# A two-layer network and a wide sigmoid head on one core: another order of the start, of the loop's small steps, and of the gathers

## The chip, the core and the metric

The kernel runs on one core of a Trainium2 chip. A core has TensorE (PE, matrix products), VectorE (DVE), ScalarE (ACT), GpSimd (POOL) and SyncE (SP), each with its own in-order program, and 16 DMA engines that they share. Engines wait for each other by semaphores. The metric is device time in microseconds (us) of one execution; less is better.

## The reference

For each of 2048 pairs (user, item) the kernel gathers two embeddings of 32 numbers, runs two layers of 128 with a relu, and makes 1250 logits. The one-hot part of the head is a lookup of a row of the head's matrix by item.

```
all_embed = jnp.concatenate([users_emb_w[users], items_emb_w[items]], axis=1)
h = jax.nn.relu(all_embed @ w1.T + b1)
h = jax.nn.relu(h @ w2.T + b2)
cross = jax.nn.one_hot(items, NUM_ITEMS, dtype=h.dtype)
head_in = jnp.concatenate([cross, h], axis=1)
return jax.nn.sigmoid(head_in @ w_head.T + b_head)
```

## The kernel before, in words

The 2048 pairs are 16 tiles of 128 (`TILES`, `LAST` = 15). The host lays an item's embedding and its row of the head side by side, so that one gathered item row has 1282 numbers.

**POOL** makes the identity `ident` and then issues for each tile two indirect DMAs: the item rows (L181, 128 x 1282 numbers) and the user rows (L185, 128 x 32). Both raise the tile's own semaphore `s_rows[t]`; a tile's embedding is complete when both have landed. From tile 4 on POOL waits for tile t-4 to have landed.

**The steps of a tile t.** Products run in fp32r, a format of reduced precision, so operands are split into a high and a low part.
- DVE `split_emb(t)` (cast L221, subtract L223) makes `emb`, high and low side by side; it waits for `s_rows[t]`.
- PE `transpose(t)` (L340) writes `ps_x`; DVE `copy_embT(t)` (L227) copies it to `embT`.
- PE `layer_1(t)` (L345, L346); ACT `relu_1(t)` (L296) makes `h1T`; PE `layer_2(t)` (L355); ACT `relu_2(t)` makes `h2T_hi` (L300) and `h2T_f` (L305); DVE `split_h2(t)` (L231) makes `h2T_lo`.
- PE's head in four passes over 1250 columns (512, 512, 226) into `acc[t % 2]` in PSUM: bias (`bias_sel` x `bias_parts`), high (`h2T_hi` x `w_hid_hi`), high-low (`h2T_hi` x `w_hid_lo`), low (`h2T_lo` x `w_hid_hi`). All are L359. The end of the low pass raises `s_acc`. Tiles 0, 14 and 15 go bank by bank instead (`bank_head`, L385 to L390), with `s_bank_acc` after each bank.
- DVE `add_part(t, i)` (L244) adds `acc` to the gathered head row, in two halves of 625 for tiles 1 to 13 (`HALVED`), in three banks otherwise. ACT `sigmoid(t, i)` (L310) follows in place, and SP stores the part (L166).

**The order** of each engine's program is written out by hand. PE has a loop over tiles 2 to 13 (`Fori`, two tiles a turn): bias pass of t, layer 1 of t+1, high pass and high-low pass of t, layer 2 of t+1, transpose of t+2, low pass of t. The programs of DVE and ACT are unrolled Python loops whose order fits this.

**The start.** PE multiplies zeros (`WARM` = 6 products of 512 columns, L395). SP loads `idx`, the head's bias, `w1T` twice and `w2T`; ACT loads b1, b2 as columns of one number per partition, and `w_hid_f` (625 KB), which ACT copies and DVE splits into `w_hid_hi` and `w_hid_lo` (`split_hidden(i)`, L213).

Of the kernel before, what the change touches and what calls it, by code (L numbers as in the profile page):

```python
# [8 lines left out]
IN_FLIGHT = 4  # L9
WARM = 6  # L10
HALVED = tuple(range(1, 14))
STORED_WHOLE = (9, 10, 11)

ALU = mybir.AluOpType
# [6 lines left out]
def rec_head_kernel(nc, pairs, user_rows, item_rows, w1T, b1, w2T, b2, w_hiddenT, b_head, out):  # L21
# [15 lines left out]
    BANKS = len(chunks)  # L37
    SPARE = BANKS * BANK - P

# [13 lines left out]
    assert B % P == 0 and H1 == P and H2 == P and 2 * K1 == P and item_rows.shape[1] == ITEM_ROW  # L53
    assert BP * BC == N and TILES > IN_FLIGHT and SPARE >= N and LAST % 2 == 1

# [6 lines left out]
    with ExitStack() as ctx:  # L62
# [6 lines left out]
        def sem(name):  # L69
            return ctx.enter_context(nc.semaphore(name))  # L70
# [7 lines left out]
        w2T_sb = sb("w2T_sb", [H1, H2], F32)  # L78
        b1_sb = sb("b1_sb", [H1, 1], F32)
        b2_sb = sb("b2_sb", [H2, 1], F32)  # L80
        w_hid_f = sb("w_hid_f", [H2, N], F32)
# [55 lines left out]
        def second_layer(t):  # L137


            return acc[1][:, SPARE:SPARE + P] if t == 0 else ps_h[:, P:2 * P]  # L140

# [8 lines left out]
        @block.sync  # L150
        def _(sp):
            sp.dma_start(idx[:], pairs_v).then_inc(s_idx, 16)
            sp.dma_start(bias_f[:], bias_v).then_inc(s_bhead, 16)
            for half in range(2):
                sp.dma_start(w1T_f[half * K1:(half + 1) * K1, :], w1T).then_inc(s_w1, 16)
            sp.dma_start(w2T_sb[:], w2T).then_inc(s_w2, 16)
            sp.wait_ge(s_const, 3)
            sp.wait_ge(s_bias_split, 2)
            for r, part in enumerate((bias_hi, bias_lo)):
                sp.dma_start(bias_parts[r:r + 1, :].bitcast(F32).rearrange("a (p c) -> a p c", p=BP),  # L160
                             part[:].bitcast(F32)).then_inc(s_bias_row, 16)

            for t in range(TILES):
                for i, (c, n) in enumerate(stores[t][:-1] if t == LAST else stores[t]):
                    sp.wait_ge(s_prob, parts_until(t) if t in STORED_WHOLE else parts_until(t - 1) + i + 1)
                    sp.dma_start(out_v[:, t * N + c:t * N + c + n], logits(t, c, n)).then_inc(s_out, 16)  # L166
            sp.wait_ge(s_out, 16 * sum(len(s) for s in stores))

        @block.gpsimd
        def _(pool):  # L170
            nc.gpsimd.memset(ident[:], 0.0).then_inc(s_zero, 1)
            pool.wait_ge(s_zero, 1)
            nc.gpsimd.affine_select(out=ident[:], in_=ident[:], compare_op=ALU.not_equal, fill=1.0, base=0,
                                    pattern=[[-1, P]], channel_multiplier=1).then_inc(s_ident, 1)
            pool.wait_ge(s_idx, 16)
            for t in range(TILES):

                if t >= IN_FLIGHT:
# [4 lines left out]
                    in_offset=bass.IndirectOffsetOnAxis(ap=idx[:, 2 * t + 1:2 * t + 2], axis=0),  # L183
                ).then_inc(s_rows[t], 16)
                nc.gpsimd.indirect_dma_start(  # L185
                    out=rows[:, at:at + UD], out_offset=None, in_=user_rows,
                    in_offset=bass.IndirectOffsetOnAxis(ap=idx[:, 2 * t:2 * t + 1], axis=0),
                ).then_inc(s_rows[t], 16)

        @block.vector  # L190
        def _(dve):
            nc.vector.memset(warm_pe[:], 0.0).then_inc(s_warm_pe, 1)  # L192
            nc.vector.memset(warm[:], 0.0).then_inc(s_const, 1)
# [64 lines left out]
            split_h2(1)
            add_part(0, 1)
            add_part(0, 2)  # L260
            split_emb(3)
            copy_embT(3)
# [18 lines left out]
        def _(act):  # L281


            act.dma_start(b1_sb[:], b1.rearrange("(p a) -> p a", a=1)).then_inc(s_b12, 16)
            act.dma_start(b2_sb[:], b2.rearrange("(p a) -> p a", a=1)).then_inc(s_b12, 16)
            act.dma_start(w_hid_f[:], w_hiddenT).then_inc(s_hidden, 16)
            act.wait_ge(s_const, 1)
# [6 lines left out]
            def relu_1(t):  # L294
                act.wait_ge(s_l1, t + 1)
                nc.scalar.activation(h1T[:], ps_h[:, 0:P], ACT.Relu, bias=b1_sb[:]).then_inc(s_h1, 1)  # L296

            def relu_2(t):
                act.wait_ge(s_l2, t + 1)
                nc.scalar.activation(h2T_hi[t % SLOTS][:], second_layer(t), ACT.Relu,  # L300
                                     bias=b2_sb[:]).then_inc(s_h2_hi, 1)
                if t >= 1:

                    act.wait_ge(s_h2_lo, t)
                nc.scalar.activation(h2T_f[:], second_layer(t), ACT.Relu, bias=b2_sb[:]).then_inc(s_h2, 1)  # L305

# [4 lines left out]

            act.wait_ge(s_b12, 32)
            relu_1(0)
            relu_2(0)
            relu_1(1)
            relu_2(1)
            sigmoid(0, 0)
            relu_1(2)
            sigmoid(0, 1)
            relu_2(2)  # L320
            sigmoid(0, 2)
# [15 lines left out]
        def _(pe):  # L337
# [40 lines left out]

            def bank_head(t, i):

                s = t % SLOTS
                c, n = chunks[i]
                if t >= SLOTS:
                    pe.wait_ge(s_sum, parts_until(t - SLOTS))
                    nc.tensor.matmul(acc[s][:, c:c + n], bias_sel[:], bias_parts[:, c:c + n], start=True, stop=False)  # L385
                pe.wait_ge(s_h2_hi, t + 1)
                nc.tensor.matmul(acc[s][:, c:c + n], h2T_hi[s][:], w_hid_hi[:, c:c + n], start=False, stop=False)  # L387
                nc.tensor.matmul(acc[s][:, c:c + n], h2T_hi[s][:], w_hid_lo[:, c:c + n], start=False, stop=False)  # L388
                pe.wait_ge(s_h2_lo, t + 1)
                nc.tensor.matmul(acc[s][:, c:c + n], h2T_lo[s][:], w_hid_hi[:, c:c + n],  # L390
                                 start=False, stop=True).then_inc(s_bank_acc, 1)

            pe.wait_ge(s_warm_pe, 1)
# [12 lines left out]
            layer_2(0, second_layer(0))  # L406
            transpose(1)

            pe.wait_ge(s_h1, 1)
            layer_1(1)  # L410
            bank_head(0, 0)
            layer_2(1)
            bank_head(0, 1)
            transpose(2)

            bias_pass(1, chunks[-1:])
            bank_head(0, 2)
            def small_beside_head(t, s):
                next_layer_1(t + 1)
                hi_pass(t, s)  # L420
                hi_lo_pass(s)

                layer_2(t + 1)
                transpose(t + 2)
                lo_pass(t, s)

            small_beside_head(1, 1)

            with pe.Fori(1, LAST // 2) as i:
                for s in range(SLOTS):  # L430
# [3 lines left out]
                    one_pass(s, bias_sel[:], bias_parts, True, False)  # L434
                    small_beside_head(t, s)
# [39 lines left out]
```

## Time and profile before

| what | value |
|---|---|
| median of the runs | 66.62 us (66.48 to 66.84, 3 runs) |
| span of the profiled execution, first to last instruction | 65.9 us |
| PE busy | 56.0 us (85%) |
| DVE busy | 43.0 us (65%) |
| ACT busy | 40.3 us (61%) |
| POOL busy | 31.2 us (47%) |
| moved by DMA | 21.85 MB, mean 332 GB/s |

The span is what the hardware profiler saw on the core. The execution's own time is not given beside it, so the runs' median is set against it: about 0.7 us more. Busy times overlap between engines.

### The profile page before, as it was taken

How to read it: one execution, taken by the hardware profiler on the slowest of the kernel's cores; microseconds unless marked ns; L12 is line 12 of the kernel's file. 1: busy time of each engine (PE TensorE's matmuls, PEld its weight loads, DVE VectorE, ACT ScalarE, POOL GpSimd, SP SyncE). 2: the span in 40 equal slices, each digit the busy share in tenths (PEclk: the TensorE clock that was granted, in tenths of full speed). 3: DMA queues.
4: the chain of work that ended last, by engine and by line, in shares of the span. 5: the costliest groups of instructions: out<-in, count | busy, mean ns of one | idle time of the engine just before them, and what ended most of it. 6: DMA issues, size and time to landing. Idle time of an engine off the chain costs nothing.

```text
span 65.9 us, 958 instructions
## 1 busy us (share of the span) xinstructions
PE 56.0 (85%) x284; PEld 44.9 (68%) x284; DVE 43.0 (65%) x111; ACT 40.3 (61%) x91; POOL 31.2 (47%) x38
## 2 busy tenths in 40 slices
PE   1999909799999999999999999999999999993000
PEld 1344207388888888888888888888888878881000
DVE  3811666134558987978879797887978879966000
ACT  0623931424256787777878768787876878978000
POOL 4287688688688678768768868800000000000000
PEclk9999998555599999999999999999999999999955
DMA  0489998998989899999999999999999999999940
GB/s 0 53 321 291 298 350 257 222 343 259 222 283 303 336 382 401 392 406 409 401 410 414 400 426 411 410 413 415 410 402 395 419 404 401 390 346 346 372 145 9
DMA packets 8367, 21.85 MB, mean 332 GB/s; under 512 B 1580, under 2 KB 2476, under 8 KB 8364
## 3 DMA queue, kind: packets, MB, share of 16 engines
q0 software_dynamic: 2816, 10.77, 46.7%
q1 hardware_dynamic: 4972, 10.29, 41.1%
q10 hardware_dynamic: 576, 0.76, 3.8%
q8 instruction: 1, 0.02, 0.1%
q14 instruction: 2, 0.02, 0.1%
HBM read 11.56 MB, written 10.24 MB: 331 GB/s over the span
## 4 chain that ended last, share of the span: by engine, by line
PE 73%; DMA 11%; ACT 2%; DVE 2%; POOL 2%; issue 2%
PE acc L359 47%; DMA rows<-user_rows,idx 8%; PE ps_h L355 6%; PE acc L387 3%; PE acc L390 3%; PE acc L388 3%; PE ps_x L340 3%; PE ps_h L346 3%; DMA idx<-pairs 3%; PE ps_h L345 3%; PE acc L385 2%; POOL rows L181 2%; ACT rows L310 1%; DVE rows L244 1%; PE acc L355 1%
## 5 line engine op out<-in xcount | busy, mean ns | idle before, releaser
L244 DVE TENSOR_TENSOR rows<-acc,rows 128x625 f32<-128x625 f32 (+2 forms) x35 | 25.8, 749 | 5.3 <-PE acc L359 3.2
L310 ACT ACTIVATE rows<-rows 128x625 f32<-128x625 f32 (+2 forms) x35 | 23.3, 678 | 0.9 <-DVE rows L244 0.9
L181 POOL DMA_INDIRECT rows<-item_rows,idx x16 | 15.3, 954 | 6.0 <-issue 4.6
L185 POOL DMA_INDIRECT rows<-user_rows,idx x16 | 15.3, 955 | 4.9 <-issue 4.9
L359 PE MATMUL acc<-bias_parts,bias_sel 128*128 128x512 f32 (+1 forms) x42 | 11.2, 373 | 0.0
L359 PE MATMUL acc<-w_hid_hi,h2T_lo 128*128 128x512 f32 (+1 forms) x39 | 10.5, 376 | 0.0
L296 ACT ACTIVATE h1T<-ps_h,b_sb 128x128 f32<-128x128 f32 x16 | 5.9, 368 | 7.1 <-PE ps_h L346 6.6
L359 PE MATMUL acc<-w_hid_hi,h2T_hi 128*128 128x512 f32 (+1 forms) x39 | 10.0, 365 | 0.0
L300 ACT ACTIVATE h2T_hi<-ps_h,b_sb 128x128 fp32r<-128x128 f32 x15 | 5.5, 369 | 7.1 <-PE ps_h L355 7.1
L359 PE MATMUL acc<-w_hid_lo,h2T_hi 128*128 128x512 f32 (+1 forms) x39 | 9.6, 354 | 0.0
L227 DVE CAST embT<-ps_x 128x128 fp32r<-128x128 f32 x16 | 4.7, 292 | 5.5 <-PE ps_x L340 5.4
L395 PE MATMUL ps_x<-warm_pe 128*128 128x512 f32 x12 | 6.8, 728 | 1.5 <-DVE warm_pe L192 1.5
L359 PEld LDWEIGHTS acc<-bias_parts,bias_sel 128*128 128x128 f32 x42 | 7.0, 194 | 1.2 <-issue 0.2
L359 PEld LDWEIGHTS acc<-w_hid_lo,h2T_hi 128*128 128x128 f32 x39 | 6.3, 189 | 1.1
L359 PEld LDWEIGHTS acc<-w_hid_hi,h2T_hi 128*128 128x128 f32 x39 | 6.4, 190 | 0.5
L359 PEld LDWEIGHTS acc<-w_hid_hi,h2T_lo 128*128 128x128 f32 x39 | 6.4, 190 | 0.5
L340 PE MATMUL ps_x<-ident,emb 128*128 128x128 f32 x16 | 4.7, 292 | 1.8 <-DVE emb L223 1.8
L355 PE MATMUL ps_h<-h1T,w2T_sb 128*128 128x128 f32 x30 | 6.1, 287 | 0.0
L395 PEld LDWEIGHTS ps_x<-warm_pe 128*128 128x128 f32 x12 | 2.8, 241 | 4.7 <-issue 3.2
L355 PEld LDWEIGHTS ps_h<-h1T,w2T_sb 128*128 128x128 f32 x30 | 4.9, 199 | 0.9
L305 ACT ACTIVATE h2T_f<-ps_h,b_sb 128x128 f32<-128x128 f32 x15 | 5.4, 363 | 0.0
L231 DVE TENSOR_TENSOR h2T_lo<-h2T_f,h2T_hi 128x128 fp32r<-128x128 f32 x16 | 4.6, 290 | 0.5 <-ACT h2T_f L305 0.4
(39 smaller groups left out, 58.1 us busy)
## 6 DMA issues: line engine op xcount, KB each, us to landing
probs<-rows SPq DMA_DIRECT2D x20, 312.5 KB
probs<-rows SPq DMA_DIRECT2D x3, 625.0 KB
probs<-rows SPq DMA_DIRECT2D x6, 256.0 KB
w_hid_f<-w_hiddenT ACTq DMA_DIRECT2D x1, 625.0 KB
rows<-item_rows,idx POOLq DMA_INDIRECT x16, 5.9
rows<-user_rows,idx POOLq DMA_INDIRECT x16, 5.9
probs<-rows SPq DMA_DIRECT2D x2, 113.0 KB
probs<-rows ACTq DMA_DIRECT2D x1, 113.0 KB
```

Of the source, the lines that this page charges most:

```text
L181: nc.gpsimd.indirect_dma_start(out=rows[:, at + UD:at + ROW], out_offset=None, in_=item_rows, in_offset=bass.IndirectOffsetOnAxis(ap=idx[: ...
L185: nc.gpsimd.indirect_dma_start(out=rows[:, at:at + UD], out_offset=None, in_=user_rows, in_offset=bass.IndirectOffsetOnAxis(ap=idx[:, 2 * ...
L227: nc.vector.tensor_copy(embT[:], ps_x[:, 0:P]).then_inc(s_embT, 1)
L244: nc.vector.tensor_tensor(logits(t, c, n), acc[t % SLOTS][:, c:c + n], logits(t, c, n), ALU.add).then_inc(s_sum, 1)
L296: nc.scalar.activation(h1T[:], ps_h[:, 0:P], ACT.Relu, bias=b1_sb[:]).then_inc(s_h1, 1)
L300: nc.scalar.activation(h2T_hi[t % SLOTS][:], second_layer(t), ACT.Relu, bias=b2_sb[:]).then_inc(s_h2_hi, 1)
L305: nc.scalar.activation(h2T_f[:], second_layer(t), ACT.Relu, bias=b2_sb[:]).then_inc(s_h2, 1)
L310: nc.scalar.activation(logits(t, c, n), logits(t, c, n), ACT.Sigmoid).then_inc(s_prob, 1)
L340: nc.tensor.transpose(ps_x[:, 0:P], emb[:], ident[:]).then_inc(s_xT, 1)
L355: nc.tensor.matmul(sums, w2T_sb[:], h1T[:], start=True, stop=True).then_inc(s_l2, 1)
L359: last = nc.tensor.matmul(acc[s][:, c:c + n], h, w[:, c:c + n], start=first, stop=end)
L395: nc.tensor.matmul(ps_x[:], warm_pe[:, 0:P], warm_pe[:], start=True, stop=True)
```

## The change

- **POOL.** The load of `w_hid_f` is issued first, by POOL and not by ACT; the memset of `ident` goes to DVE. From tile 3 on (`ITEM_FIRST`) the item gather of tile t+1 is issued ahead of the user gather of tile t.
- **Loads.** One half of `w1T` and the head's bias go from SP to ACT. b1 and b2 come in as two rows, are transposed by one small product into `ps_h`, and copied by DVE into `b12_sb`.
- **PE's start.** 3 long warm-up products, and 4 and 3 short ones of 128 columns after the first and second part of `w_hid_hi`. Bias products of tile 0 fill the time until `embT`, and its bias pass runs again after layer 1. The second layer of tile 0 goes to `ps_x`. Tile 0's head and the small steps of tile 1 are interleaved anew, with the low product of a bank apart (`bank_lo`).
- **The loop, PE.** Layer 1 of t+1 stands behind the high pass of t.
- **The loop, DVE.** Copy, first add, h2 split, second add, then the embedding split of t+2, which stood between the first add and the h2 split.
- **The loop, ACT.** The first sigmoid stands ahead of relu 1, the second ahead of relu 2, up to tile 12.
- **Before the last tiles.** Bank 0 of tile 14 stands ahead of layer 1 of tile 15, bank 1 ahead of layer 2.

```diff
-WARM = 6
+WARM = 3
+WARM_SHORT = (4, 3)
+ITEM_FIRST = 3
@@ sync
-            sp.dma_start(bias_f[:], bias_v).then_inc(s_bhead, 16)
-            for half in range(2):
-                sp.dma_start(w1T_f[half * K1:(half + 1) * K1, :], w1T).then_inc(s_w1, 16)
+            sp.dma_start(w1T_f[0:K1, :], w1T).then_inc(s_w1, 16)
@@ gpsimd
-            nc.gpsimd.memset(ident[:], 0.0).then_inc(s_zero, 1)
+            pool.dma_start(w_hid_f[:], w_hiddenT).then_inc(s_hidden, 16)
...
+            for t in range(TILES):
+                if t < ITEM_FIRST:
+                    item_gather(t)
+                if t + 1 >= ITEM_FIRST and t < LAST:
+                    item_gather(t + 1)
+                user_gather(t)
@@ vector
+            dve.wait_ge(s_b12_T, 1)
+            nc.vector.tensor_copy(b12_sb[:], ps_h[:, 0:2]).then_inc(s_b12_sb, 1)
...
             for t in range(2, LAST - 1):
-
+                copy_embT(t + 1)
                 add_part(t - 1, 0)
-                if t + 2 < TILES:
-                    split_emb(t + 2)
                 split_h2(t)
                 add_part(t - 1, 1)
-                if t + 2 < TILES:
-                    copy_embT(t + 2)
+                split_emb(t + 2)
+            copy_embT(LAST)
+            add_part(LAST - 2, 0)
             split_h2(LAST - 1)
-            add_rows(LAST - 2)
+            add_part(LAST - 2, 1)
@@ scalar
-            act.dma_start(w_hid_f[:], w_hiddenT).then_inc(s_hidden, 16)
+            act.dma_start(w1T_f[K1:2 * K1, :], w1T).then_inc(s_w1, 16)
+            act.dma_start(bias_f[:], bias_v).then_inc(s_bhead, 16)
+            act.dma_start(b12_rows[0:1, :], b1.rearrange("(a p) -> a p", a=1)).then_inc(s_b12, 16)
+            act.dma_start(b12_rows[1:2, :], b2.rearrange("(a p) -> a p", a=1)).then_inc(s_b12, 16)
...
-            for t in range(2, LAST):
-
+            for t in range(2, LAST - 2):
+                sigmoid(t - 1, 0)
                 relu_1(t + 1)
-
+                sigmoid(t - 1, 1)
+                relu_2(t + 1)
+            for t in (LAST - 2, LAST - 1):
                 sigmoid(t - 1, 0)
+                relu_1(t + 1)
                 relu_2(t + 1)
                 sigmoid(t - 1, 1)
@@ tensor
             pe.wait_ge(s_warm_pe, 1)
-            for _ in range(WARM):
-                nc.tensor.matmul(ps_x[:], warm_pe[:, 0:P], warm_pe[:], start=True, stop=True)
+            warm_up(WARM, BANK)
             pe.wait_ge(s_ident, 1)
+            pe.wait_ge(s_b12, 32)
+            nc.tensor.transpose(ps_h[:, 0:2], b12_rows[:], ident[0:2, 0:2]).then_inc(s_b12_T, 1)
+            for bank, count in enumerate(WARM_SHORT):
+                pe.wait_ge(s_hid_hi, bank + 1)
+                warm_up(count, P)
             transpose(0)
-            pe.wait_ge(s_w1_parts, 2)
-
             pe.wait_ge(s_const, 4)
             pe.wait_ge(s_bias_row, 32)
+            one_pass(0, bias_sel[:], bias_parts, True, True, chunks[:-1])
+            pe.wait_ge(s_w1_parts, 2)
+            layer_1(0)
             bias_pass(0)
-            layer_1(0)
-            bias_pass(1, chunks[:-1])
             pe.wait_ge(s_w2, 16)
             layer_2(0, second_layer(0))
+            bias_pass(1)
+            bank_hi(0, 0)
...
+                    hi_pass(t, s)
+                    next_layer_1(t + 1)
+                    hi_lo_pass(s)
+                    layer_2(t + 1)
+                    transpose(t + 2)
+                    lo_pass(t, s)
+            bank_head(LAST - 1, 0)
             next_layer_1(LAST)
-            bank_head(LAST - 1, 0)
+            bank_head(LAST - 1, 1)
             layer_2(LAST)
-            bank_head(LAST - 1, 1)
```

On DVE in the loop, from one first add to the next, the kernel before has these rows (`rows<-acc,rows` is an add, `emb` the embedding split):

```order
L244 TENSOR_TENSOR rows<-acc,rows 128x625
L221 CAST emb<-rows 128x64
L223 TENSOR_TENSOR emb<-rows,emb 128x64
L231 TENSOR_TENSOR h2T_lo<-h2T_f,h2T_hi 128x128
L244 TENSOR_TENSOR rows<-acc,rows 128x625
L227 CAST embT<-ps_x 128x128
```

The changed kernel has these, at the same place:

```order
L256 TENSOR_TENSOR rows<-acc,rows 128x625
L243 TENSOR_TENSOR h2T_lo<-h2T_f,h2T_hi 128x128
L256 TENSOR_TENSOR rows<-acc,rows 128x625
L233 CAST emb<-rows 128x64
L235 TENSOR_TENSOR emb<-rows,emb 128x64
L239 CAST embT<-ps_x 128x128
```

The two instructions of the embedding split have moved behind both adds.

On ACT in the loop, from one `h1T` (relu 1) on, before:

```order
L296 ACTIVATE h1T<-ps_h,b_sb 128x128
L310 ACTIVATE rows<-rows 128x625
L300 ACTIVATE h2T_hi<-ps_h,b_sb 128x128
L305 ACTIVATE h2T_f<-ps_h,b_sb 128x128
L310 ACTIVATE rows<-rows 128x625
```

and in the changed kernel, from one first sigmoid (`rows<-rows`) on:

```order
L321 ACTIVATE rows<-rows 128x625
L307 ACTIVATE h1T<-ps_h,b_sb 128x128
L321 ACTIVATE rows<-rows 128x625
L311 ACTIVATE h2T_hi<-ps_h,b_sb 128x128
L316 ACTIVATE h2T_f<-ps_h,b_sb 128x128
```

Each relu now has a sigmoid of the tile before ahead of it.

## Rows read from the trace of the kernel before

**Rows 1.** The page: the span, then PE's granted clock and DMA in 40 slices.

```profile
span 65.9 us, 958 instructions
...
PEclk9999998555599999999999999999999999999955
DMA  0489998998989899999999999999999999999940
```

**Rows 2.** Two stretches: length, busy time by engine, granted clock, DMA share, GB/s.

```profile
20.00:48.00 28.00, 28.00 (x171) 24.66 (x169) 23.52 (x60) 21.67 (x50) 17.41 (x19) 1.00 1.03 397
48.00:60.00 12.00, 11.74 (x67) 9.82 (x65) 9.91 (x23) 9.85 (x22) 0.00 (x0) 1.00 1.01 388
```

**Rows 3.** Timeline of one period in the loop: start, length, engine, instruction.

```profile
26.06 0.81 DVE L244 TENSOR_TENSOR rows<-acc,rows 128x625 f32<-128x625 f32 x1 [0.27 <-PE acc L359]
...
26.79 0.18 DVE L221 CAST emb<-rows 128x64 fp32r<-128x64 f32 x1
26.82 0.37 ACT L296 ACTIVATE h1T<-ps_h,b_sb 128x128 f32<-128x128 f32 x1 [0.18 <-PE ps_h L346]
...
27.00 0.23 DVE L223 TENSOR_TENSOR emb<-rows,emb 128x64 f32<-128x64 f32 x1
27.08 0.72 ACT L310 ACTIVATE rows<-rows 128x625 f32<-128x625 f32 x1
27.15 0.29 DVE L231 TENSOR_TENSOR h2T_lo<-h2T_f,h2T_hi 128x128 fp32r<-128x128 f32 x1
...
27.35 0.81 DVE L244 TENSOR_TENSOR rows<-acc,rows 128x625 f32<-128x625 f32 x1
...
28.03 0.27 PE L340 MATMUL ps_x<-ident,emb 128*128 128x128 f32 x1
...
28.34 0.29 DVE L227 CAST embT<-ps_x 128x128 fp32r<-128x128 f32 x1 [0.19 <-PE ps_x L340]
...
28.90 0.81 DVE L244 TENSOR_TENSOR rows<-acc,rows 128x625 f32<-128x625 f32 x1 [0.27 <-PE acc L359]
```

**Rows 4.** Timeline: warm-up, the transposes of tiles 0 and 3.

```profile
1.46 6.82 PE L395 MATMUL ps_x<-warm_pe 128*128 128x512 f32 x12 [1.46 <-DVE warm_pe L192]
...
9.67 0.22 DVE L223 TENSOR_TENSOR emb<-rows,emb 128x64 f32<-128x64 f32 x1
...
10.04 0.30 PE L340 MATMUL ps_x<-ident,emb 128*128 128x128 f32 x1 [1.77 <-DVE emb L223]
...
19.51 0.27 PE L340 MATMUL ps_x<-ident,emb 128*128 128x128 f32 x1
```

**Rows 5.** The chain that ended last: users of tile 0, two products of 512 columns.

```profile
4.31 5.11 DMA rows<-user_rows,idx
...
14.43 0.43 PE acc L388
...
55.44 0.23 PE acc L388
```

**Rows 6.** DMA issues from 11.8 to 11.9 us: the last number is us to landing.

```profile
rows<-user_rows,idx POOLq DMA_INDIRECT x1, 3.5
```

**Rows 7.** Timeline: the transpose of tile 15 and the end.

```profile
53.59 0.27 PE L340 MATMUL ps_x<-ident,emb 128*128 128x128 f32 x1
...
60.12 0.91 ACT L310 ACTIVATE rows<-rows 128x512 f32<-128x512 f32 x2 [0.29 <-DVE rows L244]
61.06 0.35 ACTq L334 DMA_DIRECT2D probs<-rows  x1
```

**Rows 8.** Waits of SP's queue: total, times, longest.

```profile
SPq L62 <- DMA probs<-rows: 4.4, 1, 4.4
```

**Rows 9.** DMA issues from 0.7 to 0.8 us.

```profile
idx<-pairs SPq DMA_DIRECT2D x1, 16.0 KB, 1.9
```

**Rows 10.** Waits from 54 to 66 us.

```profile
PEld ps_h L345 <- ACT h2T_f L305: 0.3, 1, 0.3
```

**Rows 11.** DMA issues from 19.2 to 19.5 us (users of tile 6).

```profile
rows<-user_rows,idx POOLq DMA_INDIRECT x1, 5.9
```

**Rows 12.** DMA issues from 40.6 to 40.8 us (items of tile 15).

```profile
rows<-item_rows,idx POOLq DMA_INDIRECT x1, 7.8
```

More of the change, by code:

```diff
@@ L53, in rec_head_kernel @@
     assert B % P == 0 and H1 == P and H2 == P and 2 * K1 == P and item_rows.shape[1] == ITEM_ROW
-    assert BP * BC == N and TILES > IN_FLIGHT and SPARE >= N and LAST % 2 == 1
+    assert BP * BC == N and TILES > IN_FLIGHT and LAST % 2 == 1
     assert all(parts_until(t) == 2 * t + 3 for t in range(LAST - 1))
@@ L107, in rec_head_kernel @@
         s_b12 = sem("s_b12")
+        s_b12_T = sem("s_b12_T")
+        s_b12_sb = sem("s_b12_sb")
         s_hidden = sem("s_hidden")
@@ L175, in _, with item_gather @@
             pool.wait_ge(s_idx, 16)
-            for t in range(TILES):
+            def item_gather(t):
                 if t >= IN_FLIGHT:
@@ L184, in _, with user_gather @@
                 ).then_inc(s_rows[t], 16)
+            def user_gather(t):
+                at = t * ROW
                 nc.gpsimd.indirect_dma_start(
@@ L188, in _ @@
                 ).then_inc(s_rows[t], 16)
+            for t in range(TILES):
[4 more added lines that the diff above has]
+                user_gather(t)
         @block.vector
         def _(dve):
+            nc.vector.memset(ident[:], 0.0).then_inc(s_zero, 1)
             nc.vector.memset(warm_pe[:], 0.0).then_inc(s_warm_pe, 1)
@@ L295, in relu_1 @@
                 act.wait_ge(s_l1, t + 1)
-                nc.scalar.activation(h1T[:], ps_h[:, 0:P], ACT.Relu, bias=b1_sb[:]).then_inc(s_h1, 1)
+                nc.scalar.activation(h1T[:], ps_h[:, 0:P], ACT.Relu, bias=b12_sb[:, 0:1]).then_inc(s_h1, 1)
             def relu_2(t):
@@ L300, in relu_2 @@
                 nc.scalar.activation(h2T_hi[t % SLOTS][:], second_layer(t), ACT.Relu,
-                                     bias=b2_sb[:]).then_inc(s_h2_hi, 1)
+                                     bias=b12_sb[:, 1:2]).then_inc(s_h2_hi, 1)
                 if t >= 1:
                     act.wait_ge(s_h2_lo, t)
-                nc.scalar.activation(h2T_f[:], second_layer(t), ACT.Relu, bias=b2_sb[:]).then_inc(s_h2, 1)
+                nc.scalar.activation(h2T_f[:], second_layer(t), ACT.Relu, bias=b12_sb[:, 1:2]).then_inc(s_h2, 1)
             def sigmoid(t, i):
@@ L391, in bank_head, with warm_up @@
                                  start=False, stop=True).then_inc(s_bank_acc, 1)
+            def bank_head(t, i):
+                if t >= SLOTS:
+                    bank_bias(t, i)
+                bank_hi(t, i)
+                bank_lo(t, i)
+            def warm_up(count, cols):
+                for _ in range(count):
+                    nc.tensor.matmul(acc[0][:, 0:cols], warm_pe[:, 0:P], warm_pe[:, 0:cols], start=True, stop=True)
             pe.wait_ge(s_warm_pe, 1)
-            for _ in range(WARM):
-                nc.tensor.matmul(ps_x[:], warm_pe[:, 0:P], warm_pe[:], start=True, stop=True)
+            warm_up(WARM, BANK)
             pe.wait_ge(s_ident, 1)
+            pe.wait_ge(s_b12, 32)
[3 more added lines that the diff above has]
+                warm_up(count, P)
             transpose(0)
-            pe.wait_ge(s_w1_parts, 2)
             pe.wait_ge(s_const, 4)
             pe.wait_ge(s_bias_row, 32)
+            one_pass(0, bias_sel[:], bias_parts, True, True, chunks[:-1])
+            pe.wait_ge(s_w1_parts, 2)
+            layer_1(0)
             bias_pass(0)
-            layer_1(0)
-            bias_pass(1, chunks[:-1])
             pe.wait_ge(s_w2, 16)
             layer_2(0, second_layer(0))
+            bias_pass(1)
+            bank_hi(0, 0)
+            pe.wait_ge(s_h2, 1)
             transpose(1)
-            pe.wait_ge(s_h1, 1)
+            bank_lo(0, 0)
+            bank_hi(0, 1)
             layer_1(1)
-            bank_head(0, 0)
+            bank_lo(0, 1)
+            bank_hi(0, 2)
+            bank_lo(0, 2)
             layer_2(1)
-            bank_head(0, 1)
+            hi_pass(1, 1)
             transpose(2)
[L416 to L427, printed above, removed]
+            hi_lo_pass(1)
+            next_layer_1(2)
+            lo_pass(1, 1)
+            layer_2(2)
+            transpose(3)
             with pe.Fori(1, LAST // 2) as i:
```

46 lines of the change are left out of this document (24 added, 22 removed).

## The prediction

> **What bounds the kernel now.** I read the page first. Its span is 65.9 us [rows 1], and the runs have a median of 66.62, so 0.7 us lie around the span; all sums below are made on the span and 0.7 is added at the end. The DMA line stands at 9 from the third slice almost to the end, and the TensorE line is at full clock but for four slices near the start and the last two [rows 1]. The windows then tell the two main stages apart. From 20 to 48 us PE is busy for the whole 28 us, and the DMA engines too (share 1.03, 397 GB/s) [rows 2]. So two things are full at once. PE takes one tile per 2.84 us (two adds of the same half of successive tiles start at 26.06 and 28.90 [rows 3]). A tile moves 128 x 1282 x 4 + 128 x 32 x 4 bytes in and 128 x 1250 x 4 out, 1.31 MB, which is 3.3 us at 397 GB/s. So until the gathers are through, PE makes output faster than it is stored and a backlog of stores grows; after that the stores have the engines alone (48 to 60 us: PE 11.74 of 12, DMA 1.01) [rows 2]. At the end both meet: ACT's last sigmoids end at 61.03 (60.12 + 0.91), its store is issued at 61.06, and SP waits 4.4 us for stores [rows 7, 8]; the span ends at 65.9, 4.87 us after the last sigmoid. That is more than twice the 1.9 us that a small lone transfer takes from issue to landing (idx) [rows 9], so some of it is backlog.
>
> For the timetable I use three marks of PE: the transpose of tile 0 at 10.04, of tile 3 at 19.51 [rows 4], of tile 15 at 53.59 [rows 7]. 19.51 + 12 x 2.84 = 53.59. The last sigmoid comes 7.44 later.
>
> **The change, part by part.** The largest part is the order in the loop, where I find a ring of waits. In the changed loop DVE goes copy, first add, h2 split, second add, embedding split (cast and subtract), and PE puts the transpose of tile t+2, which needs that embedding split, ahead of the low pass of tile t, whose end releases the next first add. All of it is now one after the other. Its length from [rows 3], start to start: first add 0.73 (26.06 to 26.79), h2 split 0.20 (27.15 to 27.35), second add 0.73 (as the first, same shape), cast 0.21 (26.79 to 27.00), subtract 0.23. The release of PE after a subtract took 0.14 to 0.15 (at tile 0: cast and subtract done at 9.89, transpose 10.04 [rows 4]). Together 2.25 from the first add to the transpose. From the transpose to the next first add it is 0.87 (28.03 to 28.90). The ring is 3.12 us. Before, the embedding split stood between the first add and the h2 split and was done by 27.23, 0.8 us before PE wanted it at 28.03; PE's own work, 2.84, was the longer.
>
> A second ring on ACT is nearly as long: the first sigmoid now stands ahead of relu 1. First add 0.81, then 0.03, sigmoid about 0.62 to the next start, relu 1 0.37, 0.05 to 0.13 to PE, layer 2 0.23, and 0.87 back: 2.98 to 3.06. It stays just behind the first. Moving layer 1 behind the high pass costs nothing, since relu 1 waits for the sigmoid anyhow.
>
> The ring acts from tile 4 to tile 15. The first period is shorter, since the low pass of tile 1 still stands ahead of the transpose of tile 3: 2.8. So tile 3 to tile 15 takes 2.8 + 11 x 3.12 = 37.1 against 34.1: **+3.0 us**.
>
> The tail: the low pass of bank 0 of tile 14 now waits for an h2 split that stands behind the add of tile 13. That split ends at 0.87 + 0.73 + 0.29 = 1.89 after the last transpose, PE goes on at 2.02, having arrived at 1.40. The stall of 0.6 replaces one of 0.3 that PE has there now (its weight load's wait for h2T_f) [rows 10]. +0.3, so 7.8 from the last transpose to the last sigmoid.
>
> The start. The new order there reaches the first add earlier by work that PE leaves for later, and what counts for the end is when tile 3 is transposed. PE warms up with 3 long products in place of 6 (now it works without a break from 1.46 to 8.28 [rows 4]) and with 7 short ones. The page shows the granted clock at half from 11.5 to 18 us after PE had stood idle for 1.77 us ahead of tile 0 [rows 1, 4]; a product of 512 columns then takes 0.43, against 0.23 at full clock [rows 5]. With less work ahead of tile 0 than now I expect half clock there too, and take it to last until the transpose of tile 1; that is a choice between full clock throughout (first rival) and half clock until tile 3, which would add 1.5 us. The Trainium skill (TensorE: Matmul & The Clock Gate, Part 1) states that the low clock is the default and activity lifts it; by that rule too fewer warm-up products are a risk, and the page's slices agree. Steps from the transpose of tile 0, at half clock: two bias products 0.86, layer 1 at 0.98 to 1.41, three bias products 1.06, layer 2 0.43, three more 1.06, two of bank 0 0.86: transpose of tile 1 at +4.8. From there at full clock: three bank passes and layer 1 and 2 of tile 1, 1.8; to relu 2 of tile 1 and through it 0.9; high pass 0.58, transpose and high-low pass 0.7, layer 1 0.2, relu 1 0.7, layer 2 0.23: +5.2. So tile 3 comes 10.0 us after tile 0.
>
> When is tile 0 transposed? Its rows landed 5.11 us after the issue of the users at 4.31 [rows 5], where the users of tile 3, asked for at 11.84, took 3.5 [rows 6]; the large load of w_hid shares the engines in between. That load now goes through POOL's queue ahead of the gathers. The bounds are 1.6 us earlier (5.11 less 3.5) and 1.6 later (0.64 MB at 397 GB/s wholly in front). POOL itself waits for idx with time to spare either way. I take 0.3 earlier, near none, since load and gather move the same bytes as before. Tile 0 at 9.7, tile 3 at 19.7 (now 19.51).
>
> The items of tile t+1 ahead of the users of tile t: POOL issues just as many gathers, items are asked for one slot (1.25 us) earlier and users one slot later, from tile 2 on. Users of tile 3: asked at 13.09, 3.5 to land, 16.6; wanted by 19. Users of tile 6, asked at 19.33 now, take 5.9 [rows 11]: now 25.2, then 26.5, wanted at 28.1 (19.7 + 2.8 + 2 x 3.12 less 0.6). 1.6 us of cover, so I cost it at nothing. If the cover is gone, DVE stands at the cast, and the adds behind it stand too. The gain from it, earlier bytes, is in the drain, which is not last here.
>
> b1 and b2 as two rows, a transpose of two columns and a copy: beside the wait for w_hid and the gathers, nothing. The memset of ident moves to DVE, about 0.2 us, ahead of waits that are longer: nothing.
>
> The sum: 19.7 + 37.1 + 7.8 = 64.6 for the last sigmoid (now 61.03). Behind it, between 2.2 (0.3 to issue and the 1.9 of a lone transfer) and today's 4.87 [rows 7, 9]. PE now makes a tile in 3.12 us and the stores alone need 0.64 MB / 388 GB/s = 1.65, so after the gathers the backlog melts: about 5.9 MB are left at 48 us, 15 us of work, done near 63, before the last sigmoid. I take 2.9. Span 67.5, time 68.2. (The Trainium skill, DMA: Bandwidth & Descriptors, "Anatomy of one DMA", gives about 2.0 us fixed and bytes / 436 GB/s. By it the last store of 0.12 MB takes 2.3, with 0.3 ahead 2.6, and the time is 67.9, called an estimate.)
>
> **The rivals.** (1) The clock stays full from the warm-up on. For it: long products at 10.2 us still ran at full clock after a pause of 1.77; against it: the clock fell soon after, and there will be less work in that stretch. Then tile 3 comes 8.4 after tile 0, 18.1, the last sigmoid at 63.0, the drain near 63.3 takes part again: span 66.2, time 66.9. (2) Late users. If gathers fall back by a slot more than I take, as the last item gather does (7.8 us [rows 12], where 5.9 left 1.6 of cover), each tile waits for the next tile's items: +1, 69.2. (3) Faster, the other side: the ring does not bind, because DVE gets through its steps faster when it works them off in this order, and the end stays with the drain. Then the earlier items fill the gaps in the gathers between 10 and 18 us (DMA line at 8 to 9 [rows 1]) and the drain ends 0.6 to 1 us earlier: 65.8. It decides if the ring is shorter than about 2.9 us, for 19.7 + 12 x 2.9 + 7.8 = 62.3 ends no later than the drain lets it. All its pieces are measured, so I give it little.
>
> **How the numbers follow.** The main case 0.46 (68.2, its own range 67.3 to 69.1), full clock 0.24 (66.9, half of it within 0.5%), late users 0.16 (69.2), no ring 0.14 (65.8). 0.5%, 0.33 us, is about what a measurement can tell. Faster: the last case and a little of the second, 0.16. Same: 0.14. Slower: 0.70. The range leaves out the fast case and the far end of late users: 66.3 to 69.4.
>
> **What would show it.** In the loop, first adds 3.1 us apart, PE idle some 0.28 before each transpose with the subtract as releaser, PE busy near 91% there. The transposes of tiles 3 and 15 near 19.7 and 56.8, the last sigmoid near 64.6. PEclk at half around tile 0. DMA below 9 in the last slices. Adds 2.84 apart would refute the ring; casts that wait for user rows would show late users.

## The result, and the profile after

The changed kernel takes **69.51 us** (median of 4 runs, 68.63 to 70.03) against 66.69 in the same job, with a ratio of 1.0377 (95% interval 1.0308 to 1.0446). The ratios, here and below, are those of the fast runs alone, while the medians have the slow runs in them, so differences between kernels are read from the ratios. By the medians the change costs 2.8 us, by the ratio 2.5. The forecast was 68.2 with a range up to 69.4: the sign was right and the size too small. The median lies 0.1 us above the range, the time by the ratio (66.69 x 1.0377 = 69.2) inside it.

The page of the changed kernel, the same lines as [rows 1]:

```profile
span 67.7 us, 982 instructions
...
PEclk9999999999999999999999999999999999999999
DMA  0589999999989999999999999999999775544990
```

This execution took 69.57 us, so 1.87 lie around its span. PE's clock never falls to its half level. The DMA line drops to 7, 5 and 4 before the end, where that of before stood at 9.

The two stretches of [rows 2]:

```profile
20.00:48.00 28.00, 27.88 (x154) 22.40 (x153) 21.39 (x55) 19.72 (x45) 17.09 (x18) 1.00 1.02 398
48.00:60.00 12.00, 11.60 (x66) 9.25 (x64) 8.88 (x22) 7.94 (x18) 0.00 (x0) 1.00 0.80 314
```

From 20 to 48 us the DMA engines are as full as before. PE has 154 instructions recorded there against 171, DVE 55 against 60, and yet PE reads as busy for 27.88 us. Part of the waiting is counted into the products' durations (a product of layer 2 reads as 326 ns on average there, 278 before), so PE's busy share hides the ring; the numbers of instructions show it, and so does the busy time of the weight loads (22.40 against 24.66). From 48 us on the stores no longer fill the DMA engines (0.80 against 1.01): the drain now has slack, and what PE loses is lost at the end too.

One period of the loop, as [rows 3] (timeline):

```profile
25.64 0.81 DVE L256 TENSOR_TENSOR rows<-acc,rows 128x625 f32<-128x625 f32 x1 [0.28 <-PE acc L373]
...
26.48 0.73 ACT L321 ACTIVATE rows<-rows 128x625 f32<-128x625 f32 x1 [0.89 <-DVE rows L256]
26.57 0.80 DVE L256 TENSOR_TENSOR rows<-acc,rows 128x625 f32<-128x625 f32 x1
27.12 0.35 ACT L307 ACTIVATE h1T<-ps_h,b_sb 128x128 f32<-128x128 f32 x1
27.29 0.18 DVE L233 CAST emb<-rows 128x64 fp32r<-128x64 f32 x1
27.50 0.23 DVE L235 TENSOR_TENSOR emb<-rows,emb 128x64 f32<-128x64 f32 x1
27.52 0.49 PE L369 MATMUL ps_h<-h1T,w2T_sb 128*128 128x128 f32 x2
27.84 0.27 PE L354 MATMUL ps_x<-ident,emb 128*128 128x128 f32 x1
28.73 0.81 DVE L256 TENSOR_TENSOR rows<-acc,rows 128x625 f32<-128x625 f32 x1 [0.28 <-PE acc L373]
```

First adds are 3.09 apart (25.64, 28.73), 2.84 before. Both rings can be read off. On DVE: add, add, cast, subtract to 27.73, transpose at 27.84, next add at 28.73. On ACT: add to 26.45, sigmoid at 26.48, relu 1 at 27.12 to 27.47, layer 2 at 27.52. They end within 0.1 us of each other: the transpose follows layer 2 by 0.32, about what it takes where no subtract is late (0.33 in a kernel below, 36.72 to 37.05), and it follows the end of the subtract by 0.11. The waits name the one on ACT (engine, line, what for: total, times, longest):

```profile
ACT rows L321 <- DVE rows L256: 11.0, 13, 1.1
...
POOL rows L180 <- DMA rows<-user_rows,idx: 3.8, 6, 1.1
...
PEld ps_h L369 <- ACT h1T L307: 3.4, 12, 0.4
```

The start (timeline; `bias_parts` holds the head's bias, `bias_f` is its load):

```profile
1.34 0.92 ACTq L295 DMA_DIRECT2D bias_f<-b_head  x1
...
4.45 0.45 DVE L209 CAST bias_hi<-bias_f 10x125 fp32r<-10x125 f32 x1 [1.20 <-DMA bias_f<-b_head]
...
6.23 0.73 SPq L159 DMA_DIRECT2D bias_parts<-bias_lo  x1
...
9.12 0.33 PE L354 MATMUL ps_x<-ident,emb 128*128 128x128 f32 x1 [0.50 <-DVE emb L235]
...
10.78 0.70 PE L373 MATMUL acc<-bias_parts,bias_sel 128*128 128x512 f32 x2 [1.34 <-DMA bias_parts<-bias_lo]
11.33 0.22 PE L359 MATMUL ps_h<-embT,w1T_hi 128*128 128x128 f32 x1
...
13.77 0.27 PE L354 MATMUL ps_x<-ident,emb 128*128 128x128 f32 x1
...
18.92 0.27 PE L354 MATMUL ps_x<-ident,emb 128*128 128x128 f32 x1
```

Here is a wait that I had not looked for. Between the transpose of tile 0 (9.12) and everything else PE stands 1.34 us for `bias_parts`. The chain that ended last goes through it:

```profile
1.34 3.08 DMA bias_f<-b_head
4.45 0.46 DVE bias_hi L209
5.31 0.87 SPq L159
6.23 4.42 DMA bias_parts<-bias_lo
```

The end, as [rows 7], and SP's last wait, as [rows 8]:

```profile
55.90 0.27 PE L354 MATMUL ps_x<-ident,emb 128*128 128x128 f32 x1
...
60.27 3.59 ACT L321 ACTIVATE rows<-rows 128x625 f32<-128x625 f32 x7
63.89 0.38 ACTq L348 DMA_DIRECT2D probs<-rows  x1
```

```profile
SPq L63 <- DMA probs<-rows: 3.3, 1, 3.3
```

Tile 15 is transposed at 55.90, the last sigmoid ends at 63.86, and the span at 67.7, 3.84 later (4.87 before).

### The profile page after: what moved, and what is told of

Its sections match the earlier page's. It is cut to its first block, busy times and chain, and to the rows that moved or that the text cites. A ratio compares the mean times of both kernels' runs of the same rounds, so it can differ in the third digit from the quotient of the medians.

```text
span 67.7 us, 982 instructions
## 1 busy us (share of the span) xinstructions
PE 58.2 (86%) x295; PEld 44.2 (65%) x295; DVE 43.7 (64%) x113; ACT 39.9 (59%) x91; POOL 31.6 (47%) x38
## 4 chain that ended last, share of the span: by engine, by line
PE 67%; DMA 11%; DVE 8%; ACT 4%; SPq 1%; issue 1%; ACTq 1%
PE acc L373 45%; PE ps_h L369 9%; DMA bias_parts<-bias_lo 7%; DVE rows L256 6%; DMA bias_f<-b_head 5%; PE ps_x L354 3%; PE ps_h L360 2%; ACT rows L321 2%; PE acc L413 2%; PE ps_h L359 2%; PE acc L403 1%; SPq L159 1%; PE acc L407 1%; ACT h2T_hi L311 1%; ACTq L294 1%
## 5 line engine op out<-in xcount | busy, mean ns | idle before, releaser
L373 PE MATMUL acc<-w_hid_lo,h2T_hi 128*128 128x512 f32 (+1 forms) x39 | 10.2, 370 | 0.0
L424 PE MATMUL acc<-warm_pe 128*128 128x128 f32 (+1 forms) x20 | 6.9, 505 | 1.6 <-DVE warm_pe L202 1.6
L369 PE MATMUL ps_h<-h1T,w2T_sb 128*128 128x128 f32 x30 | 7.2, 322 | 0.1
L424 PEld LDWEIGHTS acc<-warm_pe 128*128 128x128 f32 x20 | 3.5, 232 | 3.7 <-issue 2.1
```

The lines of the kernel that those rows point to most:

```text
L369: nc.tensor.matmul(sums, w2T_sb[:], h1T[:], start=True, stop=True).then_inc(s_l2, 1)
L373: last = nc.tensor.matmul(acc[s][:, c:c + n], h, w[:, c:c + n], start=first, stop=end)
L424: nc.tensor.matmul(acc[0][:, 0:cols], warm_pe[:, 0:P], warm_pe[:, 0:cols], start=True, stop=True)
```

## The experiments

Twelve runs in three jobs. "T3" and "T15" are the transposes of those tiles in the profiled execution, in us; period is the usual distance of transposes in the middle of the loop. The first row is from the job of the result; in the two other jobs of this table the kernel before had a median of 66.64.

| kernel | median us | ratio to before | T3 | T15 | period |
|---|---|---|---|---|---|
| changed | 69.51 | 1.0377 (1.0308 to 1.0446) | 18.92 | 55.90 | 3.08 |
| changed, old gather order | 68.78 | 1.0368 (1.0308 to 1.0428) | 20.04 | 56.91 | 3.08 |
| changed, old ACT order | 69.21 | 1.0387 (1.0312 to 1.0462) | 18.27 | 55.12 | 3.08 |
| changed, old DVE order | 69.51 | 1.0405 (1.032 to 1.049) | 18.36 | 55.73 | 3.09 |
| changed, old ACT and DVE | 68.30 | 1.028 (1.0214 to 1.0345) | 19.50 | 54.91 | 2.96 |
| changed, old PE, ACT, DVE loops | 67.91 | 1.0186 (1.0125 to 1.0247) | 19.34 | 54.70 | 2.85 |
| before, looked at again | 66.43 (one run) | none | 16.95 | 52.48 | 2.84 |
| before, new PE, ACT, DVE loops | 67.23 | 1.011 (1.0068 to 1.0153) | 16.72 | 54.38 | 3.08 |
| before, items first | 66.39 | 0.9966 (0.9935 to 0.9998) | 19.98 | 54.56 | 2.85 |

**The gather order alone, undone.**

```diff
-ITEM_FIRST = 3
+ITEM_FIRST = 16
```

> The changed kernel with the old order of gathers (items and users of a tile one after the other). Theory (the loop's ring of waits costs, the gathers' order does not): adds of the loop stay 3.09 us apart, tile 15 transposed within 0.5 us of 55.9, time 69.3 to 69.8. Rival (users behind the next items make each tile late): 1 us or more faster, below 68.6.

68.78 against 69.51, below the 69.3 to 69.8 expected, but with ratios whose intervals nearly coincide: no difference can be told. Adds and transposes are as far apart as before the edit. Tiles 3 and 15 are late in the table because the profiled execution (70.54 us) was granted only half clock, 0.50 from 12 to 14 us: tile 1 comes 5.89 us after tile 0 there, against 4.65, and tile 15 36.87 after tile 3, against 36.98. The new waits of POOL's item gathers for rows (3.8 us in the changed kernel, above) are gone here, and nothing came of it: POOL was ahead. No cost and no gain of items-first can be seen in this kernel.

**One ring undone, then the other, then both.**

```diff
 ACT, tiles 2 to 12 (first edit)
-                sigmoid(t - 1, 0)
                 relu_1(t + 1)
-                sigmoid(t - 1, 1)
+                sigmoid(t - 1, 0)
                 relu_2(t + 1)
+                sigmoid(t - 1, 1)
 DVE, tiles 2 to 13 (second edit)
                 add_part(t - 1, 0)
+                split_emb(t + 2)
                 split_h2(t)
                 add_part(t - 1, 1)
-                split_emb(t + 2)
```

> The changed kernel with ACT's old order in the loop (relu 1 ahead of the first sigmoid, relu 2 ahead of the second), DVE as changed. If the ring through DVE is as long as worked out, the period is still 3.05 to 3.12 and the time 69.2 to 69.7. If only the ring through ACT binds, the period falls to 2.85 and the time by 2 us or more.

> The changed kernel with DVE's old place for the embedding split (behind the first add), ACT as changed. If the ring through ACT binds too, the period stays at 3.05 to 3.09 and the time at 69.2 to 69.6. If only the ring through DVE binds, the period falls to 2.85 and the time by 2 us or more.

> The changed kernel with both old orders in the loop, all else as changed. Theory of the rings: period 2.84 to 2.90, tile 15 transposed 2 to 2.8 us earlier than 55.9, and the time falls by 1.5 to 2.8 us to 66.7 to 68; it falls by less than PE wins if stores are last by then. Rival (start, tail or what lies around the span is what costs): within 0.5 us of 69.5.

Either edit alone leaves the period at 3.08 or 3.09 and the time where it was (medians 69.21 and 69.51, ratios 1.0387 and 1.0405 against 1.0377). In the timeline the binding ring changes. With the old ACT order PE has layer 2 done early and the transpose follows the subtract:

```profile
46.76 0.81 DVE L256 TENSOR_TENSOR rows<-acc,rows 128x625 f32<-128x625 f32 x1 [0.28 <-PE acc L373]
...
48.51 0.49 PE L369 MATMUL ps_h<-h1T,w2T_sb 128*128 128x128 f32 x2
48.62 0.23 DVE L235 TENSOR_TENSOR emb<-rows,emb 128x64 f32<-128x64 f32 x1
48.90 0.33 PE L354 MATMUL ps_x<-ident,emb 128*128 128x128 f32 x1
```

With the old DVE order the subtract is done at 48.54, a whole microsecond before the transpose, and layer 2 waits for relu 1 behind the sigmoid:

```profile
48.21 0.73 ACT L321 ACTIVATE rows<-rows 128x625 f32<-128x625 f32 x1 [0.56 <-DVE rows L256]
...
48.31 0.23 DVE L235 TENSOR_TENSOR emb<-rows,emb 128x64 f32<-128x64 f32 x1
...
48.84 0.35 ACT L307 ACTIVATE h1T<-ps_h,b_sb 128x128 f32<-128x128 f32 x1
49.24 0.30 PEld L369 LDWEIGHTS ps_h<-h1T,w2T_sb 128*128 128x128 f32 x2 [0.27 <-ACT h1T L307]
...
49.57 0.27 PE L354 MATMUL ps_x<-ident,emb 128*128 128x128 f32 x1
```

With both undone the period falls to 2.96 and the last sigmoid comes 1.0 us earlier (62.85, 63.86). The median falls by 1.2 us, the ratio by 0.0097, which is 0.6 us with an interval from about 0 to 1.3. Both are less than the 1.5 expected at least, and the period does not reach 2.84. The timeline says why:

```profile
36.10 0.78 PE L373 MATMUL acc<-w_hid_lo,h2T_hi 128*128 128x512 f32 x3
...
36.30 0.37 ACT L307 ACTIVATE h1T<-ps_h,b_sb 128x128 f32<-128x128 f32 x1 [0.77 <-PE ps_h L360]
...
36.72 0.49 PE L369 MATMUL ps_h<-h1T,w2T_sb 128*128 128x128 f32 x2
```

ACT has stood 0.77 us when layer 1 comes, and relu 1 is through at 36.67. The high-low pass, all that PE has between layer 1 and layer 2 now, is a little shorter than that. I take it that layer 1 behind the high pass costs 0.1 us a tile as soon as the sigmoid no longer hides it; the next kernel tries that.

**All three loops undone in the changed kernel, or put alone into the kernel before.** The first adds to the two edits above that layer 1 stands ahead of the high pass again; the second leaves start, tail and gathers as they were.

```diff
 PE, the first of the two
-                    hi_pass(t, s)
                     next_layer_1(t + 1)
+                    hi_pass(t, s)
                     hi_lo_pass(s)
 PE, the second
-                    small_beside_head(t, s)
+                    hi_pass(t, s)
+                    next_layer_1(t + 1)
+                    hi_lo_pass(s)
+                    layer_2(t + 1)
+                    transpose(t + 2)
+                    lo_pass(t, s)
```

> The changed kernel with the old orders in the loop on all three engines (also layer 1 ahead of the high pass); start, tail and gathers as changed. Theory: period 2.84 in place of 2.96 (both orders of DVE and ACT restored), tile 15 transposed 1.1 to 1.4 us earlier than 54.9, time 67.0 to 67.8. Rival (late rows or DMA set the period by then): 2.96 stays, 68.3.

> The kernel before with nothing but the changed orders inside the loop on PE, DVE and ACT. Theory of the rings: period 3.08, tile 15 transposed 2.6 to 3.0 us later, time 1.3 to 2.6 us above before (68.0 to 69.2), less than PE loses since before has a backlog of stores at its end. Rival (the start and the tail are what costs): within 0.5 us of before.

The usual period is 2.85 in the one and 3.08 in the other, so the place of layer 1 is worth the 0.1 us a tile (2.96, 2.85). In the time it does not show. Tile 15 comes at 54.70, 0.2 us earlier than with the two edits and not 1.1 to 1.4, since DVE stands 2.7 us in all for late rows in this profile (1.00 at tile 5); and the ratios 1.028 and 1.0186 have intervals that overlap.

Out of the changed kernel the loops take 1.3 us by the ratios (1.0377 to 1.0186; medians 69.51 and 67.91), and the last sigmoid moves by 1.2 (63.86 to 62.66). Into the kernel before they bring only 0.7 (ratio 1.011, interval 0.5 to 1.0; medians 66.64 and 67.23), below the 1.3 expected at least, although the last sigmoid comes 1.8 us later there (59.91, 61.72) and tile 15 1.9 (52.48, 54.38). That 0.7 and 1.3 differ is not clear of noise; that the price in the kernel before is less than its 1.8 us of lateness is. The share and rate of DMA from 48 to 60 us go with it. First the kernel before (its second look, below), then the one with the new loops (windows):

```profile
48.00:60.00 12.00, 10.62 (x61) 8.89 (x59) 9.64 (x22) 9.74 (x22) 0.00 (x0) 1.00 1.03 395
```

```profile
48.00:60.00 12.00, 12.00 (x67) 9.94 (x67) 9.43 (x22) 9.10 (x22) 0.00 (x0) 1.00 0.96 371
```

Before, the stores were still full (1.03) and the span ended 4.7 us after the last sigmoid (59.91, 64.6); with the new loops 3.1 us after it (61.72, 64.8). The backlog took up the difference. With the new start as well there is less of a backlog (0.80 in the changed kernel, 0.88 with the old loops in it), and the span moves by all of what the last sigmoid does (66.1, 67.7).

**The kernel before once more.**

> The kernel before once more, for a second profile. The first one's span of 65.9 us lies above the 64.3 to 65.4 that the timed runs of this kernel gave, at a granted clock of 0.921 against 0.97 to 0.99. Theory: the stretch at half clock near the start is not usual; here the clock is above 0.97, tile 3 is transposed near 18.4 and not 19.5, and the span is 64.3 to 65.4. Rival: half clock stays and the spans differ by the drain of stores.

The page, the start and the longest of the waits for rows:

```profile
span 64.6 us, 958 instructions
...
PEclk9999999999999999999999999999999999999855
DMA  0489989988978999999999999999999999999980
```

```profile
9.82 0.30 PE L340 MATMUL ps_x<-ident,emb 128*128 128x128 f32 x1 [0.58 <-DVE emb L223]
11.86 0.27 PE L340 MATMUL ps_x<-ident,emb 128*128 128x128 f32 x1
...
16.95 0.27 PE L340 MATMUL ps_x<-ident,emb 128*128 128x128 f32 x1
19.79 0.27 PE L340 MATMUL ps_x<-ident,emb 128*128 128x128 f32 x1
...
23.23 0.20 DVE L221 CAST emb<-rows 128x64 fp32r<-128x64 f32 x1 [1.75 <-DMA rows<-user_rows,idx]
...
23.74 0.33 PE L340 MATMUL ps_x<-ident,emb 128*128 128x128 f32 x1 [0.94 <-DVE emb L223]
```

The time was 66.43, so 1.8 us lie around the span. There is no stretch of half clock at the start, tile 3 comes at 16.95 and not at 19.51 [rows 4], earlier than the 18.4 expected, and then rows are late: from tile 4 to tile 5 it takes 3.95 us, to tile 6 another 3.18, where 2.84 is usual. The execution that I had made the sum on, span 65.9, was about 1.2 us longer than the usual one.

**Items first, alone on the kernel before.**

```diff
+            for t in range(TILES):
+                if t < ITEM_FIRST:
+                    item_gather(t)
+                if t + 1 >= ITEM_FIRST and t < LAST:
+                    item_gather(t + 1)
+                user_gather(t)
```

> The kernel before with nothing but the changed order of gathers. Theory: POOL's wait for tile t-3 now comes into force and the users come a slot later, 0.2 to 1.0 us slower (66.8 to 67.6). Rival, and my prediction's reading: no cost, or 0.3 to 1 us faster by earlier bytes, since before ends with the drain.

66.39, ratio 0.9966: perhaps 0.2 us faster, hardly to be told from nothing, and not the loss that was expected. POOL's wait does come into force (3.0 us in 5 waits). In the profiled execution (67.12 us) it is not free either: the users of tile 2, asked for a slot (1.25 us) later, let DVE stand 2.71 us and PE 1.55, and tile 3 comes at 19.98.

**The bias load and the tail.** The last job was disturbed: in each of its profiles the engines stand for most of some 30 us between 12 and 49 us, in waits that the profile puts down to `remote` or `issue`, which name no engine or transfer of the core, and the kernel before took 96.4 us too. So its absolute times say nothing; what follows are details inside its profiles, and ratios within the job. The first kernel is the one with the old loops, and loads the head's bias second on SP; the second has the old tail (layer 1 of tile 15 ahead of bank 0 of tile 14, layer 2 ahead of bank 1, and the orders on DVE and ACT that go with it) in place of that; the third has both.

```diff
+            sp.dma_start(bias_f[:], bias_v).then_inc(s_bhead, 16)
-            act.dma_start(bias_f[:], bias_v).then_inc(s_bhead, 16)
```

> The changed kernel with the old loop orders and with the head's bias loaded second by SP, as before, and not by ACT behind half of w1T. Theory (PE's first real products wait for bias_parts, 1.3 us in the changed kernel): that wait goes, tile 1 is transposed near 12.6 in place of 14.1, tile 3 near 18.0 in place of 19.3, time 66.8 to 67.5 against 67.9. Rival (gathers set the pace of the first tiles): tile 3 stays above 19 and the time within 0.3 us of 67.9.

> The changed kernel with the old loop orders and the old order of the last tiles on PE, DVE and ACT. Theory: from the transpose of tile 15 to the last sigmoid 7.4 us in place of 7.95, time 67.2 to 67.7 against 67.9. Rival (the drain is last): 7.4 too, but the time within 0.2 us of 67.9.

> Old loop orders, early bias and old tail together; what is left of the change is the rest of the start and the order of gathers. Theory: the parts add up, 66.3 to 67.1, within 0.7% of the kernel before. Rival (something else in the start costs): above 67.3.

The timeline of the third:

```profile
9.17 0.33 PE L354 MATMUL ps_x<-ident,emb 128*128 128x128 f32 x1 [0.75 <-DVE emb L236]
9.27 0.71 PE L373 MATMUL acc<-bias_parts,bias_sel 128*128 128x512 f32 x2
...
12.48 0.27 PE L354 MATMUL ps_x<-ident,emb 128*128 128x128 f32 x1
```

The bias products follow the transpose at once, and tile 1 is transposed 3.31 us after tile 0 (9.17, 12.48) against 4.65 in the changed kernel: all of the 1.34 comes back there. In the first kernel the bias products went ahead as well (layer 1 at 0.80 us after the transpose, against 2.21), but then ACT stood 2.01 us ahead of relu 2 of tile 0 (0.64 in the changed kernel), and tile 1 came 4.69 after tile 0; since the third kernel has the same start and not this wait, I put it down to the disturbance. From tile 1 on the profiles are of no use for the start.

The undisturbed profiles settle the bias. Six kernels have the new start and the late bias, and PE's wait for `bias_parts` differs from one profile to the next:

| kernel | wait for `bias_parts` | tile 0 to tile 1 | less the wait |
|---|---|---|---|
| changed | 1.34 | 4.65 | 3.31 |
| changed, old ACT order | 0.78 | 4.08 | 3.30 |
| changed, old DVE order | 1.36 | 4.66 | 3.30 |
| changed, old ACT and DVE | 2.01 | 5.32 | 3.31 |
| changed, old PE, ACT, DVE loops | 1.48 | 4.78 | 3.30 |
| changed, old gather order (half clock) | 1.47 | 5.89 | 4.42 |

At full clock the distance is 3.3 us plus the wait each time, and 3.31 where the bias is early.

The tail from the transpose of tile 15 to the end of the last sigmoid takes 7.96 us in the first (83.73 to 91.69), and 7.43 and 7.41 with the old tail: 0.5 us. The medians were 100.52, 98.62 and 99.07, with ratios of 1.0151 (1.0071 to 1.0232, from two runs) for the bias and 1.0232 (1.0174 to 1.029) for the tail, and none for the third. Beside the 1.0186 of the kernel that they start from, that is no clear gain for either, and under this disturbance it can't be weighed.

**The kernel before with items first and the load of `w_hid_f` by POOL**, `ident` set by DVE:

```diff
+            pool.dma_start(w_hid_f[:], w_hiddenT).then_inc(s_hidden, 16)
-            act.dma_start(w_hid_f[:], w_hiddenT).then_inc(s_hidden, 16)
```

> The kernel before with two parts of the change: items ahead of users, and w_hid loaded first by POOL (memset of ident on DVE). Theory: rows of tile 0 land some 0.6 us sooner as in the changed kernel, tile 0 is transposed near 9.2 in place of 9.8, time 65.9 to 66.4, a version at least as fast as both. Rival (the drain and the gathers set the end, the start is hidden): 66.4 to 66.8.

Ratio 0.9842 (0.9781 to 0.9903) in that same disturbed job, 95.09 us. Tile 0 was not early, 10.56 in place of the 9.2 expected: POOL asks for the first items at 2.90, as before (2.91), and not at 2.60 as in the changed kernel, where `idx` lands after 1.6 us and not 1.9. Whether it is a gain in an undisturbed execution was not tried.

## Why the prediction was right in its sign and short in its size

| term | predicted | measured |
|---|---|---|
| transpose of tile 0 | 9.7 | 9.12 |
| tile 0 to tile 3 | 10.0 | 9.80 |
| tile 3 to tile 15 | 37.1 | 36.98 |
| tile 15 to the end of the last sigmoid | 7.8 | 7.96 |
| last sigmoid to the end of the span | 2.9 | 3.84 |
| around the span | 0.7 | 1.87 |
| sum | 68.2 | 69.57 (the profiled execution) |

**The step that failed is the first one: "0.7 us lie around the span".** I took a profiled span and the runs' median for the same execution. They weren't: executions with both recorded have 1.8 to 1.9 us around the span (66.43 and 64.6; 69.57 and 67.7). This is 1.2 of the 1.4 us that are missing (69.57 against 68.2). The other errors of the table add up to only 0.2 (the drain +0.9, the tail +0.2, tile 0 -0.6, the rest -0.3), and that they do is luck. In other words the baseline of the sum was about 1.2 us longer than the median, so the difference that I forecast from it, 1.6, was too small by the same amount.

**The drain** was 3.84 against 2.9. The backlog had melted as I said (DMA share 0.80, then 4s in the slices), yet SP waited 3.3 us for the last stores, where a lone transfer takes 1.9 [rows 9]; 3.84 is also 1.2 more than the 2.6 that I had worked out from a page of the Trainium skill (DMA: Bandwidth & Descriptors, "Anatomy of one DMA"). That section is about DMAs issued by GpSimd, and the last store is issued by ACT. What is in the 3.84 was not taken apart.

**The ring in the loop** was right: its two rings, its length (mean of the 11 periods behind the first 3.12 predicted, 3.115 measured, (55.90 - 21.63) / 11), and which steps it has. That the two values agree to 0.01 is partly luck: the usual period is 3.08 or 3.09, and a few are longer. The order of the two rings was wrong: the second, put at 2.98 to 3.06, is level with the first (3.08 with the one, 3.09 with the other), and in the changed kernel it is the one that PE waits for. So the sign that I had named, PE idle ahead of each transpose with the subtract as releaser and 91% busy, did not appear. Undoing one ring shows the other at once. That layer 1 behind the high pass "costs nothing, since relu 1 waits for the sigmoid anyhow" holds only under the second ring; without it it is 0.1 us a tile.

**The start** came out for a wrong reason. Half clock from tile 0 to tile 1 didn't occur in the profile of the changed kernel: 1.2 GHz was granted nowhere, so the clock of the first rival was right. It did occur in one with the same start (old gather order), so it was a matter of the execution. By that rival tile 3 comes 8.4 us after tile 0; it came 9.80 after, since PE waited 1.34 us for the bias, whose load I had not costed at all. It went from second on SP to second on ACT, behind half of `w1T`; the cast of it ran at 4.45 and not at 3.04, the last store into `bias_parts` was issued at 6.23 and not at 4.53, and that landed 4.42 us later, at 10.65. Before, the bias was there when PE first asked for it. An error of 1.6 (10.0 less 8.4) and one of 1.3 nearly cancelled, which is luck. Tile 0 itself came 0.6 earlier than forecast; its users were asked for at 3.91 and not at 4.31 [rows 5]. Against the usual execution of before (tile 0 at 9.82, tile 3 at 16.95) the new start is 0.7 us earlier at tile 0 and 2.0 later at tile 3. Nearly all of the 2.7 lost between lies ahead of tile 1, which is transposed 4.65 us after tile 0 (2.04 before); from tile 1 to tile 3 it is 5.15 and 5.09. With the bias early the first of these is 3.31, and without the wait it is 3.30 or 3.31 in every profile at full clock. So the bias takes 1.34 and the order of the steps that now stand ahead of tile 1 the other 1.27; this second part is what is left over, and no run undoes it alone.

**Items ahead of users** at no cost: right by the time, on both kernels, and the casts of the changed kernel wait only 0.5 us in all for user rows, so the rival of late users is out. The cover was worked out for tiles 3 and 6; in the one profile where it ran short it was tile 2. **The tail** +0.3: it is +0.5, shown by the old tail in two kernels.

Where the 3.8% (2.5 us) come from, by kernels: the loops 1.9% (1.3 us, old loops in the changed kernel), the rest 1.9% (1.2 us), of which the tail (0.5 on the marks), the bias (1.34) and the order of the start are parts seen in profiles but not priced in undisturbed time. By marks against the repeated look at before: tile 0 -0.70, tile 0 to 3 +2.67, to tile 15 +1.45 (it would be +2.9 but for the late rows in before), tail +0.53, drain -0.86; together the 3.1 us between the spans.

## What to carry to other kernels

Before a sum is made on one profiled execution, ask whether its span plus what usually lies around a span gives the median; if not, the baseline is off, and every difference with it. When an order of waits is changed, write down the ring on every engine: here two rings of 3.1 us lay on top of each other, so undoing either alone showed nothing, and a true cause could have been dismissed. And a lateness on the path has no fixed price: the same loops made the last sigmoid 1.8 us later and the time only 0.7 where a backlog of stores stood behind them, and 1.2 and 1.3 where there was less of it. Of a load that changes its queue, follow what depends on it to the last consumer, however small it is.

## What the runs showed of the hardware that I had not expected

- The granted clock at the start isn't fixed by the kernel, nor by the longest pause of PE alone. The kernel before fell to half from 11.5 to 18 us in one profile, after a pause of 1.77 us ahead of tile 0 [rows 1, 4], and stayed full in another, with a pause of 0.58. The changed kernel, with 3 long warm-up products instead of 6, stayed full over its wait of 1.34 us for the bias. With the old gather order, which leaves PE's program as it is, the clock was at half (0.50) from 12 to 14 us after such a wait of 1.47; with both orders undone it stayed full over one of 2.01.
- The copy of the bias's low part (one row of 1250 numbers) into `bias_parts`, issued at 6.23 among gathers and the load of `w_hid_f`, took 4.42 us to land, where `idx` on idle queues took 1.9 [rows 9].
- In one job all four profiled kernels stood for most of some 30 us in the first half, and the kernel before, without a profile there, took 96.4 us where 66.6 is usual. Why stays open.
